# Moving one group of dense feed-forward work and halving dense matmuls in a fused decoder layer

## What is computed

```python
N = B * S
k = max(MIN_CAPACITY, ceil(N * CAPACITY_FACTOR / E))
xt = x.reshape(N, D)
scores = jax.nn.softmax(xt @ Wr, axis=-1)
G, idx = jax.lax.top_k(scores.T, k)
X_in = xt[idx]
h = jax.nn.gelu(jnp.einsum('ekd,edh->ekh', X_in, W1) + b1[:, None, :], approximate=False)
X_e = jnp.einsum('ekh,ehd->ekd', h, W2) + b2[:, None, :]
contrib = (G[..., None] * X_e).reshape(E * k, D)
out = jnp.zeros((N, D), dtype=x.dtype).at[idx.reshape(-1)].add(contrib)
return out.reshape(B, S, D)
```

## Time and profile before

| | us |
|---|---|
| median of 3 runs | 623.18 |
| lowest and highest run | 622.03, 630.46 |
| profiled execution, first to last instruction (span) | 585.1 |
| median less span | 38.1 |
| PE, DVE, ACT, POOL busy | 549.5, 417.1, 327.3, 260.2 |

### The profile page before, as it was taken

How to read it: one execution, slowest core, us unless ns; L and a number is a source line. 1 busy time by engine, 2 the same in 40 slices (tenths; PEclk the granted TensorE clock), 3 DMA queues, 4 the chain that set the end, 5 groups by cost and what they waited for, 6 DMA issues and landing times.

```text
span 585.1 us, 11240 instructions
## 1 busy us (share of the span) xinstructions
PE 549.5 (94%) x3477; PEld 427.6 (73%) x3477; DVE 417.1 (71%) x1051; ACT 327.3 (56%) x670; POOL 260.2 (44%) x368
## 2 busy tenths in 40 slices
PE   8999999999999999999999898998999999999880
PEld 7868787888888788788878676566676575668530
DVE  3686786787687688668877875788758845656753
ACT  3577776767777677776767543442333525443133
POOL 4123524434352443435243430002777777777732
PEclk9999999999999999999999998998999999999985
DMA  7033442232234023423312404900223443665652
GB/s 242 2 82 91 135 117 52 96 109 97 47 115 134 25 83 115 112 50 115 104 60 65 150 10 144 304 2 11 55 57 106 138 129 121 191 194 163 221 185 108
DMA packets 62151, 63.43 MB, mean 108 GB/s; under 512 B 11809, under 2 KB 48930, under 8 KB 61858
## 3 DMA queue, kind: packets, MB, share of 16 engines
q1 hardware_dynamic: 58096, 55.37, 30.8%
q0 software_dynamic: 3584, 7.58, 4.6%
q10 hardware_dynamic: 434, 0.02, 0.0%
HBM read 36.85 MB, written 26.08 MB: 108 GB/s over the span
## 4 chain that ended last, share of the span: by engine, by line
PE 77%; DVE 13%; ACT 4%; issue 2%; POOL 1%; DMA 1%; POOLq 0%; DVEq 0%; ACTq 0%
PE PS L1577 17%; PE PS L1635 10%; PE PS L1607 9%; PE PS L1908 8%; PE PS L1930 7%; PE PS L1623 5%; PE PS L1821 4%; PE PS L1831 4%; DVE pc L1395 2%; DVE csum L1158 1%; ACT shared L891 1%; DVE cmax L1147 1%; PE PS L1681 1%; PE PS L1675 1%; PE PS L1667 1%
## 5 line engine op out<-in xcount | busy, mean ns | idle before, releaser
L767 POOL TENSOR_TENSOR pn<-pc,crcp 128x512 f32<-128x512 f32 (+1 forms) x93 | 80.4, 891 | 69.3 <-DVE crcp L1161 69.3
L1035 ACT ACTIVATE shared<-PS,b1T 128x512 f32<-128x512 f32 x88 | 60.5, 687 | 85.7 <-PE PS L1821 49.5
L807 POOL DMA_INDIRECT shared<-table,idx x56 | 54.3, 970 | 64.5 <-DVE idx L1402 48.0
L1607 PE MATMUL PS<-shared,x1T 128*128 128x512 f32 (+1 forms) x192 | 72.4, 513 | 1.2 <-ACT x1T L906 1.0
L817 POOL DMA_INDIRECT spread<-pn,idx x56 | 62.0, 1107 | 17.6 <-issue 15.6
L1607 PEld LDWEIGHTS PS<-shared,x1T 128*128 128x128 f32 x192 | 35.0, 189 | 37.6 <-issue 35.2
L862 ACT ACTIVATE shared<-PS 128x308 f32<-128x308 f32 x120 | 47.5, 428 | 25.5 <-PE PS L1577 25.2
L1147 DVE TENSOR_REDUCE cmax<-PS 128x16 f32<-128x1232 f32 x31 | 44.7, 1441 | 20.8 <-PE PS L1607 20.4
L1158 DVE TENSOR_REDUCE csum<-pc 128x16 f32<-128x1232 f32 x31 | 44.4, 1431 | 19.4 <-ACT pc L874 19.4
L1908 PE MATMUL PS<-pT,w 128*128 128x512 f32 x112 | 53.6, 611 | 3.3 <-ACT pT L1030 3.3
L1930 PEld LDWEIGHTS PS<-w,shared 128*128 128x128 f32 x448 | 51.7, 192 | 3.6 <-issue 3.1
(11 more groups left out here) (209 smaller groups left out, 1208.1 us busy)
## 6 DMA issues: line engine op xcount, KB each, us to landing
spread<-zeros SPq DMA_DIRECT2D x112, 128.0 KB, 2.0
shared<-spread SPq DMA_DIRECT2D x56, 256.0 KB, 4.3
xboth<-in_x SPq DMA_DIRECT2D x16, 256.0 KB, 2.7
w<-in_W SPq DMA_DIRECT2D x2, 1792.0 KB, 9.2
rest<-stage SPq DMA_DIRECT2D x56, 52.0 KB
table<-x SPq DMA_DIRECT2D x16, 128.0 KB, 1.9
fin<-table SPq DMA_DIRECT2D x1, 2048.0 KB, 18.2
out_x<-fin SPq DMA_DIRECT2D x8, 256.0 KB, 2.0
```

The source lines that it names most:

```text
L767: pool.tensor_tensor(pn[:, e, at_pn:at_pn + n * (b - a)].rearrange("p (h k) -> p h k", h=n), pc[:, e, :].rearrange("p (h k) -> p h k", h=H ...
L807: pool.indirect_dma_start(xg[:, e % 3, h, :], None, table, bass.IndirectOffsetOnAxis(ap=idx[:, e, h:h + 1], axis=0)).then_inc(gathered[e % ...
L1035: act.activation(hid[:, c, 512 * h:512 * h + 512], PS[:, HID_BANKS[k % len(HID_BANKS)], :], ACT.Gelu, bias=b1T[:, bias:bias + 1]).then_inc ...
L1607: i = pe.matmul(PS[:, n, 0:b - a], x1T[:, e, :], A[:, 2 * A_SLOT[phase] + e, a:b], start=True, stop=True)
```

## The change

- The dense matmuls of 512 columns are issued as two of 256 columns, and a result piece as two halves of two matmuls. `dense(n)` now counts such halves. The calls have twice the old number, but for those named next.
- `dense(BEFORE_GATES)` with 4 halves (two old pieces) stands ahead of the gates' transposes. All later calls of the routing find the count two pieces further. To make up for that the call behind `prefix(1, E)` has 10 halves in place of seven pieces.
- `TAIL` ties group 7 to the last listed expert, 6. Its hidden pieces come behind that expert's second layer, its result pieces behind those, in PSUM bank 7. ACT's copy and DVE's `dense_add` of group 7 move to the end of their orders ahead of the last norm, on DVE behind all of `add_landed`. The last `fin` matmul (chunk 7) waits for it.

```diff
-        TAIL = {1: IN_ROUTING, 2: IN_ROUTING + 1}
+        TAIL = {1: IN_ROUTING, LISTED - 1: IN_ROUTING + 1}
...
+        def dense_bank(g):
+
+            return 7 if g == GROUPS_OF_FOUR - 1 else 1 + (g % 2 if g < IN_ROUTING else 1)
...
+            dense_copy(GROUPS_OF_FOUR - 1)
...
             add_landed(LISTED - 2, 0, B // 4)
+            dense_add(GROUPS_OF_FOUR - 1, B // 4 * (LISTED - 1))
...
-                pe.matmul(PS[:, HID_BANKS[k % len(HID_BANKS)], :], w1d[:, c * P:(c + 1) * P],
-                          xall[:, 4 * g:4 * g + 4, :].rearrange("p b t -> p (b t)"), start=True, stop=True).then_inc(hid_full, 1)
...
+                i = pe.matmul(PS[:, HID_BANKS[k % len(HID_BANKS)], 2 * P * half:2 * P * (half + 1)], w1d[:, c * P:(c + 1) * P],
+                              xall[:, 4 * g + 2 * half:4 * g + 2 * half + 2, :].rearrange("p b t -> p (b t)"),
+                              start=True, stop=True)
...
             pe.wait_ge(consts, CONSTS)
+            pe.wait_ge(wd_in, 16 * 2)
+            dense(BEFORE_GATES)
             pe.wait_ge(gates_done, 3)
...
-            dense(2)
+            dense(PER_ROUND)
...
-            dense(7)
+            dense(10)
             make_list(1)
...
-            pe.wait_ge(hid_done, hidden_before(LISTED - 1) + 2 * FC)
             pe.wait_ge(idx_done, LISTED)
+            for s in range(4):
+                for half in range(2):
+                    dense_result(hidden_before(LISTED), GROUPS_OF_FOUR - 1, 1, s, half)
             pe.wait_ge(ye_done, blocks_through(LISTED - 1, SB - 1))
             for c in range(B // 4):
                 pe.wait_ge(landed_added, B // 4 * (LISTED - 2) + c + 1)
+                if c == B // 4 - 1:
+                    pe.wait_ge(dense_added, GROUPS_OF_FOUR)
```

More of the change, by code:

```diff
@@ L29 @@
 GROUPS_OF_FOUR = B // 4
+BEFORE_GATES = 4
+PER_ROUND = 4
 IN_ROUTING = 6
@@ L485, in hidden_before, with dense_piece @@
             return FC * IN_ROUTING + 2 * FC * e + FC * sum(e > k for k in TAIL)
-        TAIL = {1: IN_ROUTING, 2: IN_ROUTING + 1}
+        TAIL = {1: IN_ROUTING, LISTED - 1: IN_ROUTING + 1}
         CONSTS = 21
+        def dense_piece(n):
+            g, j = divmod(n - FC, 2 * FC)
+            if n < FC:
+                return "hidden", 0, n
+            if g == IN_ROUTING - 1:
+                return "result", g, j
+            return ("hidden", g + 1, j // 2) if j % 2 == 0 else ("result", g, j // 2)
+        def dense_bank(g):
+            return 7 if g == GROUPS_OF_FOUR - 1 else 1 + (g % 2 if g < IN_ROUTING else 1)
         SETUP = [("fold", 0)] + [("M", g) for g in range(4)] + [("N", g) for g in range(4)]
@@ L1036, in gelu, with dense_copy, behind_dense @@
                                bias=b1T[:, bias:bias + 1]).then_inc(hid_done, 1)
-            def dense_copy(g, h):
+            def dense_copy(g):
                 act.wait_ge(dense_full, g + 1)
-                act.activation(xall[:, 4 * g:4 * g + 4, :].rearrange("p b d -> p (b d)"), PS[:, 1 + h, :],
+                act.activation(xall[:, 4 * g:4 * g + 4, :].rearrange("p b d -> p (b d)"), PS[:, dense_bank(g), :],
                                ACT.Copy).then_inc(dense_out, 1)
-            for g in range(IN_ROUTING + 1):
-                if g < IN_ROUTING:
-                    for c in range(FC):
-                        gelu(FC * g + c, g % 2, c, FC * DENSE + c)
-                if g:
-                    dense_copy(g - 1, (g - 1) % 2)
+            def behind_dense(first, end):
+                for n in range(first // 2, end // 2):
+                    kind, g, j = dense_piece(n)
+                    if kind == "hidden":
+                        gelu(FC * g + j, g % 2, j, FC * DENSE + j)
+                    elif j == 3:
+                        dense_copy(g)
+            behind_dense(0, FC * 4 * IN_ROUTING)
             for e in range(LISTED):
@@ L1485, in _ @@
                 if e < 2:
-                    for k in range(IN_ROUTING // 2 * e, IN_ROUTING // 2 * (e + 1)):
+                    for k in range(IN_ROUTING // 2 * e, IN_ROUTING // 2 if e == 0 else IN_ROUTING):
                         dense_add(k, 0)
@@ L1816, in _, with dense_hidden, dense_result @@
                 pe.wait_ge(free[k], n)
-            def dense_hidden(k, g, h, c):
-                if k >= len(HID_BANKS):
+            def dense_hidden(k, g, h, c, half):
+                if half == 0 and k >= len(HID_BANKS):
                     pe.wait_ge(hid_done, k - len(HID_BANKS) + 1)
-                pe.matmul(PS[:, HID_BANKS[k % len(HID_BANKS)], :], w1d[:, c * P:(c + 1) * P],
-                          xall[:, 4 * g:4 * g + 4, :].rearrange("p b t -> p (b t)"), start=True, stop=True).then_inc(hid_full, 1)
-            def dense_result(k, g, h, s):
-                if s == 0:
+                i = pe.matmul(PS[:, HID_BANKS[k % len(HID_BANKS)], 2 * P * half:2 * P * (half + 1)], w1d[:, c * P:(c + 1) * P],
+                              xall[:, 4 * g + 2 * half:4 * g + 2 * half + 2, :].rearrange("p b t -> p (b t)"),
+                              start=True, stop=True)
+                if half:
+                    i.then_inc(hid_full, 1)
+            def dense_result(k, g, h, s, half):
+                if s == 0 and half == 0:
                     pe.wait_ge(hid_done, k)
@@ L1829, in dense_result @@
                         pe.wait_ge(dense_out, g - 1)
-                for c in range(FC):
-                    i = pe.matmul(PS[:, 1 + h, s * P:(s + 1) * P], hid[:, c, 512 * h + s * P:512 * h + (s + 1) * P],
+                for c in range(FC // 2 * half, FC // 2 * (half + 1)):
+                    i = pe.matmul(PS[:, dense_bank(g), s * P:(s + 1) * P], hid[:, c, 512 * h + s * P:512 * h + (s + 1) * P],
                                   w2d[:, c, :], start=(c == 0), stop=(c == FC - 1))
-                if s == 3:
+                if s == 3 and half:
                     i.then_inc(dense_full, 1)
@@ L1878, in _ @@
             prefix(0, 1)
-            dense(4)
+            dense(8)
             def make_list(e):
@@ L1952, in _ @@
                     for s in range(4):
-                        dense_result(hidden_before(e), TAIL[e - 1], 1, s)
+                        for half in range(2):
+                            dense_result(hidden_before(e), TAIL[e - 1], 1, s, half)
                 if e < LISTED - 1:
@@ L1970, in _ @@
                     for c in range(FC):
-                        dense_hidden(hidden_before(e) + 2 * FC + c, TAIL[e], 1, c)
-            pe.wait_ge(hid_done, hidden_before(LISTED - 1) + 2 * FC)
+                        for half in range(2):
+                            dense_hidden(hidden_before(e) + 2 * FC + c, TAIL[e], 1, c, half)
             pe.wait_ge(idx_done, LISTED)
+            for s in range(4):
+                for half in range(2):
+                    dense_result(hidden_before(LISTED), GROUPS_OF_FOUR - 1, 1, s, half)
             pe.wait_ge(ye_done, blocks_through(LISTED - 1, SB - 1))
```

21 lines of the change are left out of this document (8 added, 13 removed).

## The result

The changed kernel takes 635.33 us (median of 4 runs, 632.58 to 640.74) beside 623.9 us for the kernel before (4 runs, 622.03 to 630.46). The ratio is 1.0188, with a 95% interval from 1.0147 to 1.0229: slower by some 11.5 us. Ratios compare the fast runs alone, while medians and their differences are of all runs. I had forecast 623.1 us, with a range up to 626.0, so the result lies outside it.

A forecast was written before the change was run, and what follows sets the result against it. The prediction took POOL's 112 indirect DMAs to pace the whole expert stage, with PE's time covered. Its terms, -0.5 - 0.1 + 0.5 + 0 + 0 + 0, made -0.1 us on a span of 585.1, so 623.1 us, range 620.4 to 626.0.

The forecast's parts named there:

- The 38.1 us left as they are: Whole kernel: the 38.1 us between profiled span and measured median were carried over unchanged into the forecast.
- Group 7 leaves: Experts 2 and 3: with group 7 gone, POOL waits less for results; -0.5 us, ends 0 and -0.5.
- DVE's add leaves POOL's stretch: Expert stage: five DVE instructions move behind POOL's last issue, so a scatter is less disturbed; -0.1 us, ends 0 and -0.3.
- Two pieces ahead of the transposes: Routing: at low clock they delay the transposes 2.1 us, two stalls of 1.56 go; +0.5 us, ends -1.2 and +2.1.
- rival 2: Gates' transposes: clock already up for the pieces ahead of them, -1.2 in place of +0.5, giving 621.4 us; chance 0.16.
- Halving: Dense passes: cutting each in two costs nothing that shows; 0 us, upper end 0.6.
- List 1: Before list 1: two pieces fewer delay nothing unless idle lets the clock fall; 0 us, ends 0 and +0.8.
- The new tail: Behind expert 6: group 7's work and add fit before the landed chunks by 0.4 us; 0, or +1.2 without PE's lead.
- The lead: Up to expert 6's second-half transposes: PE gets at most 3.9 us ahead, ending its last second layer near 546.2.
- signs of being right: POOL's DMAs take 149 to 151 us, PE idles some 5 us before expert 6's second-half transposes, transposes start 1.9-2.1 later.
- Rival 3: Tail: idle before expert 6's second-half transposes lowers the clock, norm up to 1.2 us late; 624.3 us (to 625.1), chance 0.26.
- Rival 1: Expert stage: PE sets the pace, so removing group 7's 8.8 us there gives about 614.9 us; chance 0.06.

The follow-up runs named there:

- all_third: The whole change again, built from the kernel before, without splitting a result piece into two calls; 595.1 us against 587.7, ratio 1.0116.
- control: The kernel before, unchanged, run for a second profile; 621.3 us (one run) against 623.8.
- move_gates: The change without its halving: group 7 moved and two dense pieces ahead of the gates' transposes; 594.4 us against 587.8 for the kernel before, ratio 1.0124.
- tail_short: The whole change with group 7's second layer cut from 16 matmuls to 4; 591.7 us against 587.7 for the kernel before, ratio 1.0047.
- gates_only: Kernel before with only two dense pieces put ahead of the gates' transposes and two fewer before list 1; 628.2 us against 623.8, ratio 1.0067.
- half_gates: The change without the move of group 7: halving and the gates' pieces; 590.1 us against 587.7 for the kernel before, ratio 1.0016.
- half_gates_again: The change without the move of group 7, run in another set; 590.4 us against 586.5 for the kernel before, ratio 1.0053.
- all_again: The whole change again, built from the kernel before, without splitting a result piece into two calls; 636.0 us against 622.0, ratio 1.0296.
- gates_only_again: Only the two dense pieces ahead of the gates' transposes, on another chip; 631.6 us against 622.0 for the kernel before, ratio 1.0191.
- the two doubled kernels: Kernel before with listed experts' first-layer matmuls issued as two of 256 columns, run twice; 587.2 us against 587.8 (1.0004), 587.2 against 586.5 (1.0011).
- half_only: Kernel before with only the halving: each dense hidden matmul issued as two of 256 columns; 627.9 us against 623.8, ratio 1.0084.
- move_only: Kernel before with only group 7 moved behind the last listed expert; 630.6 us against 623.8, ratio 1.0133.
- move_only_again: Only group 7 moved behind the last listed expert, in another set; 630.6 us against 622.0 for the kernel before, ratio 1.0195.
- tail5: Kernel before with group 7 behind expert 5 instead of expert 2, one wait more, DVE's add of it left out; 627.8 us against 622.0, ratio 1.0123.
- tail5b: Kernel before with group 7 behind expert 5, DVE's add of it included; 587.7 us against 587.7, ratio 0.9998.

## Why the prediction was wrong

**What bounds.** That POOL's 112 indirect DMAs pace the expert stage holds at the lower level: 149.5 us from first to last start in the profile of before, 149.6 in all_third. At the upper level, where the result was measured, it doesn't: 182.5 us in control and 186.4 in the changed kernel, 31.6 and 34.5 of them waits for scaled results that came late.

**The 38.1 us left as they are.** This was the first wrong step. I took the distance between span and median for something outside the program, though nothing in the profile said so. control shows all but 1.8 us of it to be time inside the expert stage at the upper level, and the profile to be one of the lower. It meant that my slack (PE covered by POOL) was read where PE had most of it.

**Group 7 leaves: -0.5.** The sign was right and the size small: the last scatter of move_gates starts 147.3 us after the first gather instead of 149.5, 2.1 us of gain. But in all_third it is 149.6 and in tail_short 150.3 us, no gain. Either way it was worth nothing, since POOL no longer set the end.

**DVE's add leaves POOL's stretch: -0.1.** No run separates it.

**Two pieces ahead of the transposes: +0.5.** Nine traces hold this edit, and they fall into two groups. In five (the changed kernel, gates_only, half_gates, half_gates_again, tail_short) the first gather comes 47.95 to 47.97 us behind L1772, against 46.91 to 47.10 in the eleven kernels without the edit: +0.9 to +1.0. In four (all_again, all_third, gates_only_again, move_gates) it comes at 46.91 to 46.93: nothing. There the clock rose during the two pieces, which took 3.37 to 3.49 us instead of 3.76: rival 2, but without its gain of 1.2. The transposes moved by 2.14 us in gates_only as forecast, and the first round's wait was gone but for 0.08. The second round's 0.53 was 0.20 in control already, so it had nothing to give back there.
The Trainium skill ("TensorE: Matmul & The Clock Gate", Part 1) says that the release comes at a moment which shifts between runs. That agrees with the two groups, down to 3.37 us and at 3.76 us for the same two pieces.

**Halving: 0.** Right at the lower level, by the two doubled kernels and by half_only's own stretch. At the upper level half_only costs 4.1 us, which this term doesn't explain; that it lies in late signals and pauses is read from one profile.

**List 1: 0, ends 0 and +0.8.** I chose the wrong end. The chain that I had described (idle before the list, clock falls, a piece takes nearly twice as long) happened in half_gates, half_gates_again and tail_short (the 1.05 us that I had for a piece is that of one ahead of the list; inside it was 1.14): gather 1 waits 0.96 us longer, and list 2 another 0.7 to 0.95. "The clock did not fall before in this stretch" was no argument, since the edit itself takes out the two pieces that kept PE busy there. With the +0.9 this makes some 2.6 us, of the 2.4 and 3.9 that the two runs of half_gates cost. In all_third and move_gates, whose early pieces were the quick ones, gather 1 is on time (0.33 us); no run shows why the two go together.

**The new tail: 0.** This is the step that failed most. I let group 7's results end at 555.0, its add at 559.2, and then counted "PE's last `fin` matmul, two passes of 0.474". But PE issues in order, and all sixteen `fin` passes stand behind group 7's second layer: 7.03 us, not 0.95. By my own numbers 555.0 + 7.03 = 562.0 was already behind the landing at 560.5. Before the change these passes ran in the time in which PE waited for landings anyway.
The lead was the other half of it. I had PE end the last second layer 3.9 us earlier than before (546.2 instead of 550.1). Counted from the first gather it ends at 147.2 us in all_third and at 144.1 in before, so it came 3.1 us later. The last gather for expert 6 was issued 128.6 us behind the first instead of 125.4, which no run explains. It landed later than issue + 2.6 us: issued at 538.51, PE could go on at 542.76, 4.25 us later, with the DMA engines at 0.97 to 1.01 of their time. And the clock fell in the idle time, which cost 2.8 us in all_third, 1.2 in move_gates and 1.6 in tail_short.
Summed for all_third by the starts of PE's groups, from the last transpose to the landed passes: group 7 took 8.27 us (556.95 to 565.22); the slow second layer 2.79 more; the idle times of 1.52 and 2.16 us that PE had there before were filled, -3.68; closer packing and the shorter `fin` row give -0.73. That makes 6.65, and 7.0 with the transposes, which ended 0.36 us later. Counted from the first gather the landed passes start 572.09 - 409.94 = 162.15 us in, against 561.12 - 405.93 = 155.19: 6.96 us in place of my 0.
At the upper level the same order costs more, by another wait. The changed kernel has no idle before the transposes and no slow second layer, so of my signs of being right the new idle isn't there and neither is POOL's stretch of 149 to 151 us. But group 7 takes 602.91 - 587.89 = 15.0 us, 5.0 of them the wait for a Gelu on ACT, and from the last scatter's start to the end it is 40.4 us against control's 31.1.

**The rivals.** Rival 3 named the idle of 4.9 us before the transposes (move_gates has 2.90 + 1.96) and the slow clock behind it, and it was right at the lower level. It priced them at 1.2 us, because it was worked on the same wrong count of passes. The measured kernel, at the upper level, has neither. Rival 1, that PE sets the pace, was called refuted by POOL's gaps. At the upper level POOL's gaps do grow, but taking 8.8 us of PE's work out of the stage gained nothing that can be relied on: POOL's stretch is 186.7 us in move_only, 179.0 in move_only_again and 182.5 in control, and group 7 came back at the end.

**What stays open.** At the upper level the parts alone cost 4.1, 4.4 to 9.6 and 6.8 to 8.7 us, tail5 5.8, and the whole 11.5 to 14: they don't add up. The tail (8.6 us in all_again, 9.3 in the changed kernel's profile) carries most of the whole. That two other arrangements lose 4 us or more there (halved passes, group 7 behind expert 5), where tail5b and the doubled first layers are free at the lower level, is measured but not explained. Neither is what delays the signals or stops PE: no chip with pauses came up for the kernels that change the number of passes in the expert stage, and every run on record has a recorded span, so a part of the recording in it isn't ruled out.

## What to carry to other kernels

Work put "into the slack at the end" of an in-order engine pushes back everything queued behind it: count every instruction that follows in program order, not the one that depends on it. An idle stretch that an edit opens has two prices, the idle itself and the half-speed work after it, so work that keeps TensorE busy before a dependent burst isn't free to remove. And when the profiled span doesn't match the measured time, find out where the difference is before pricing anything by slack.

## What the runs showed of the hardware

One program has two levels on different chips, 586 to 588 and 622 to 624 us, and the difference lies in one stage, where POOL's stretch is 182.5 instead of 149.5 us. Signals of finished PE work come late there (12.3 us at list 4 in control, 0.8 before), and PE stops at steps of 0.71 us, at first at the full granted clock. The DMA engines are full at one such place (1.05 at 463 us) and a quarter busy at another, where PE waits for ACT and ACT for a signal:

```profile
509.15 3.73 PE L1831 MATMUL PS<-w2d,shared 128*128 128x128 f32 x32
...
517.94 0.60 ACT L1041 ACTIVATE xall<-PS 128x512 f32<-128x512 f32 x1 [7.91 <-remote]
...
520.77 3.49 PE L1908 MATMUL PS<-pT,w 128*128 128x512 f32 x4 [6.17 <-ACT shared L1035]
```

```profile
515.00:516.00 1.00, 0.00 (x0) 1.00 0.26 70
...
517.00:518.00 1.00, 0.00 (x0) 0.51 0.27 70
```

ACT's copy needs the 32 passes that ended at 512.88 and starts 5.1 us later.

The Trainium skill ("Runtime: NRT & Kernel Launch", section "Instruction fetch mechanics") says that TensorE's instructions are refilled in blocks by DMA, and that this is mostly hidden. Both traces, control's and that of before, list 20 packets on one queue of the kind "instruction" (0.33 MB) and 17 on another, so their number doesn't tell a chip with pauses from one without. No run here shows whether they have a part in it.

In eleven of the twenty profiles the granted clock is lower in the first 20 us, 0.91 on the mean in three and 0.74 to 0.77 in eight, instead of 1.00. Everything after it starts some 2.5 us later in the three and some 4.5 in the eight. The runs of the kernel before on one chip lie 5 to 8 us apart at the lower level, as much as the effects that are weighed here, so that single profiles had to be compared from the first gather on and not by their spans.
